# Emitting the input transposes of a sandwich block one tile later in the first attention's epilogue

## Chip, cores, metric

The kernel runs on one Trainium2 chip, on its 8 cores, one batch element of 2048 tokens on each. No data pass between the cores. The metric is device time in microseconds (us) of the slowest core.

## What is computed

The reference is one layer with two attentions and an expert stage. Cut to what matters:

```python
x = x + layernorm(attn(layernorm(x)))          # 16 heads of 64, causal, S = 2048, D = 1024
y = layernorm(x)
z = layernorm(y) * ln1_g + ln1_b               # goes into the second attention
y = y + attn2(z)                               # same shape
y = y + moe(layernorm(y) * ln2_g + ln2_b)      # 8 experts of 1024 -> 4096 -> 1024, gelu, top 2
out = x + layernorm(y)
```

All eight experts are computed for every token and weighted with the gate, which is zero for six of them.

## The kernel before

The program is written out by hand for five queues (TensorE, VectorE, ScalarE, GpSimd, SyncE); `kb.em` appends an instruction to one queue, `kb.wt`, `kb.consume` and `kb.reuse` append the waits. No scheduler moves anything: each engine works in the order in which the Python code emits.

A first stage normalizes the input tile by tile (16 tiles `tt` of 128 tokens), transposes it on TensorE and keeps it in T1, with the features on the partitions. Then comes `emit_attention` (L400), once for the first attention and once for the second. It projects K (L422) and V (L454) for all tokens, and then goes over four query blocks `qs` of 512 tokens. In a block it

- projects Q (L494): 8 groups of 8 matmuls of 512 columns, into the four PSUM banks `pb[0..3]` by turns, each evacuated by ScalarE (L504);
- runs 8 head pairs: scores (L567, masks L578), exponentials on ScalarE (L594), products with V (L615, L621, L625), and an epilogue of each pair (L511 to L545);
- for its four tiles multiplies with the output weights (L660: 16 matmuls, two halves of 8, into banks 0 and 1 or 2 and 3 by turns), and calls the epilogue `epi` of the tile: `epi1` (L672) in the first attention, `epi2` (L727) in the second.

`epi1` is a long chain for one tile: VectorE adds the bias into the buffer scrY (L679, twice), takes the layernorm statistics (`ln_stats`, L252: L256, L257, L258 on VectorE, then Ln and Exp at L260 and L261 on ScalarE), normalizes into scrZ (L690), adds the residual x that a DMA brought (L695), spills the sum x1 to memory, takes statistics a second time, copies mean and scale (L703, L704), and normalizes into scrY again (L706). Last `transpose8` (L265) transposes the eight 128x128 parts of scrY on TensorE (L273), four into bank 4 and four into bank 5, and ScalarE moves them from there into T1 (L718), where the second attention finds its input. There is one scrY: the next tile's first L679 waits until the transposes have read it. T1's part of this query block has been read by the block's Q projection by then.

Every VectorE and ScalarE instruction that is emitted as serial also waits for the one before it on its own engine. `load_bias_bcast` (L341), between the two attentions, brings a bias row by DMA into the buffer RSTG, spreads it over the partitions by two matmuls (L348; a float matmul has two records) into banks 4 and 5, and VectorE copies them out (L357). It is called twice, and the second DMA waits for the first copies.

The expert stage (L953 on) follows the second attention and a normalizing stage; neither is touched.

Of the kernel before, what the change touches and what calls it, by code (L numbers as in the profile page):

```python
# [92 lines left out]
def build_nc():  # L93
# [33 lines left out]
    with ExitStack() as ctx:  # L127
# [30 lines left out]
        kb = KB()  # L158
# [8 lines left out]
        scrY = T5[:, 5120:6144]  # L167
# [39 lines left out]
        r_afm = [Res() for _ in range(NQS)]  # L207
# [9 lines left out]
        r_scrY = Res()  # L217
# [16 lines left out]
        def dma(e, dst, src, res=None, waits=(), dkey=None):  # L234
            for w in waits:
                kb.wt(e, w)
            if res is not None:
                kb.reuse(e, res)
            if dkey is None:
                if res is not None:  # L240
                    dkey = dkeys.setdefault(id(res), "d%d" % len(dkeys))
                else:
                    anon_ctr[0] += 1
                    dkey = "a%d" % anon_ctr[0]
            tok = kb.emd(e, lambda E, d=dst, s=src: E.dma_start(out=d, in_=s), dkey)  # L245
            if res is not None:
                kb.produce(res, tok)
            return tok
# [122 lines left out]
        for tt in range(NT):  # L371
# [3 lines left out]
            m, s, tok_s = ln_stats(xr, waits=(tokd,))  # L375
# [8 lines left out]
            qs = tt // 4  # L384
# [12 lines left out]
                kb.produce(r_afm[qs], [("v", kb.cnt["v"]), ("s", kb.cnt["s"])])  # L397

        spill_toks = []
        def emit_attention(wq_h, wk_h, wv_h, wout_h, bq8c, bkc, epi, first):  # L400
            wsrc = lambda w: w.rearrange("(kc p) d -> p kc d", p=128)
            tok_wq = dma("g", wq_sb.rearrange("p (kc d) -> p kc d", d=1024), wsrc(wq_h), res=r_wq)
            for rr, half_res in ((0, r_whalfA), (1, r_whalfB)):
# [3 lines left out]
                        kb.reuse("g", rc)  # L407
                dma("g", dstA, wsrc(wk_h)[:, rr * 4:(rr + 1) * 4, :], res=half_res)
            tok_wo = dma("g", wo_sb.rearrange("p (kc d) -> p kc d", d=1024), wsrc(wout_h), res=r_wo)

            for c in range(NPAIR):
                kb.reuse("v", r_kfm[c])
# [72 lines left out]
            for qs in range(NQS):  # L485
                kb.reuse("v", r_qsl)
                for c in range(NPAIR):
# [18 lines left out]
                        func=AF.Identity, bias=bq8c[:, c:c + 1], scale=0.125), inc=1, serial=False)  # L506
                    kb.used(r_pb[bank], tv)
                kb.produce(r_qsl, ("s", kb.cnt["s"]))

                nkt = 4 * qs + 4  # L510
                def emit_pair_epilogue(p, rbT, rbb):  # L511
# [137 lines left out]
                for i in range(4):  # L649
                    tt = qs * 4 + i  # L650
                    banks = (2 * (i % 2), 2 * (i % 2) + 1)
                    toks = []
                    for ds in range(2):
                        bank = banks[ds]
                        kb.reuse("t", r_pb[bank])
                        kb.consume("t", r_wo)
                        tk = None
                        for c in range(NPAIR):
                            kb.consume("t", r_ctx[c])
                            tk = kb.em("t", lambda E, c=c, i=i, ds=ds, bank=bank: E.matmul(  # L660
                                out=pb[bank][:],
                                lhsT=ctxsb[:, c * 512 + i * 128:c * 512 + i * 128 + 128],
                                rhs=wo_sb[:, c * 1024 + ds * 512:c * 1024 + ds * 512 + 512],
                                start=(c == 0), stop=(c == NPAIR - 1)), inc=(1 if c == NPAIR - 1 else 0))
                        for c in range(NPAIR):
                            kb.used(r_ctx[c], tk)
                        kb.used(r_wo, tk)
                        kb.produce(r_pb[bank], tk)
                        toks.append(tk)
                    epi(tt, banks, toks)  # L670

        def epi1(tt, banks, toks):  # L672
            qs = tt // 4
            kb.consume("v", r_bob)
            kb.reuse("v", r_scrY)
            ty = None
            for ds in range(2):
                kb.wt("v", toks[ds])
                ty = kb.em("v", lambda E, ds=ds, b=banks[ds]: E.scalar_tensor_tensor(  # L679
                    out=scrY[:, ds * 512:(ds + 1) * 512], in0=pb[b][:], scalar=1.0,  # L680
                    in1=bob[:, ds * 512:(ds + 1) * 512], op0=OP.mult, op1=OP.add), inc=1)
                kb.used(r_pb[banks[ds]], ty)
                kb.used(r_bob, ty)
            kb.produce(r_scrY, ty)
            m, s, tok_s = ln_stats(scrY)
            sl = tt % 2
            xr = T7[:, sl * 1024:(sl + 1) * 1024]
            tokd = dma("q", xr, x_r[tt], res=r_xr[sl])
            kb.wt("v", tok_s)
            tz = scrz_write(lambda E: E.tensor_scalar(  # L690
                out=scrZ, in0=scrY, scalar1=bn2[:, 0:1], scalar2=tstat[:, 1:2],
                op0=OP.subtract, op1=OP.mult))
            kb.used(r_scrY, tz)
            kb.wt("v", tokd)
            tx1 = kb.em("v", lambda E, xr=xr: E.tensor_tensor(  # L695
                out=xr, in0=scrZ, in1=xr, op=OP.add), inc=1)
            scrz_used(tx1)
            tok_sp = dma("q", x1s_r[tt], xr, waits=(tx1,))
            spill_toks.append(tok_sp)
            kb.used(r_xr[sl], tok_sp)  # L700
            m, s, tok_s = ln_stats(xr, waits=(tx1,))
            kb.wt("v", tok_s)
            kb.em("v", lambda E, tt=tt: E.tensor_copy(out=m1s1[:, tt:tt + 1], in_=bn2[:, 0:1]))  # L703
            tms = kb.em("v", lambda E, tt=tt: E.tensor_copy(out=m1s1[:, 16 + tt:17 + tt], in_=tstat[:, 1:2]), inc=1)  # L704
            kb.reuse("v", r_scrY)
            t1 = kb.em("v", lambda E, xr=xr, tt=tt: E.tensor_scalar(  # L706
                out=scrY, in0=xr, scalar1=m1s1[:, tt:tt + 1], scalar2=m1s1[:, 16 + tt:17 + tt],
                op0=OP.subtract, op1=OP.mult), inc=1)
            kb.produce(r_scrY, t1)
            kb.used(r_xr[sl], t1)  # L710

            def evac_h1(c, pap, eng, tt=tt):
                if eng == "v":
                    return kb.em("v", lambda E, c=c, pap=pap: E.tensor_scalar(
                        out=T1[:, c * 2048 + tt * 128:c * 2048 + tt * 128 + 128], in0=pap,
                        scalar1=PPB[:, 32 + c:33 + c], scalar2=PPB[:, 40 + c:41 + c],
                        op0=OP.mult, op1=OP.add), inc=1, serial=False)
                return kb.em("s", lambda E, c=c, pap=pap: E.activation(  # L718
                    out=T1[:, c * 2048 + tt * 128:c * 2048 + tt * 128 + 128], in_=pap,
                    func=AF.Identity, scale=PPB[:, 32 + c:33 + c],  # L720
                    bias=PPB[:, 40 + c:41 + c]), inc=1, serial=False)

            transpose8(scrY, t1, evac_h1, src_res=r_scrY, engines=("s", "s"))
            if tt % 4 == 3:
                kb.produce(r_afm[qs], [("v", kb.cnt["v"]), ("s", kb.cnt["s"])])

        def epi2(tt, banks, toks):  # L727
            kb.consume("v", r_bob)
# [94 lines left out]
        for tt in range(NT):  # L823
# [17 lines left out]
            m, s, tok_s = ln_stats(u_sl(tt, 0, 1024), waits=(tu,))  # L841
# [21 lines left out]
            if pend_gm[0] is not None:  # L863
# [4 lines left out]
                       src_res=r_t2s, engines=("s", "s"))  # L868
# [244 lines left out]
```

How the kernel before makes its waits and increments, by code:

```python
        def runner(eng, e):  # L1040
            for fn, inc in kb.ops[e]:
                if isinstance(fn, tuple):
                    if fn[0] == "WAIT":
                        eng.wait_ge(sems[fn[1]], fn[2])
                    elif fn[0] == "DMA":
                        instr = fn[1](eng)
                        instr.then_inc(sems[fn[2]], 16)
                    continue
                instr = fn(eng)
                if inc:
                    instr.then_inc(sems[e], inc)
```

## Time and profile before

| | us |
|---|---|
| three timed runs | 6350.97, 6714.02, 6923.64 |
| their median | 6714.02 |
| the profiled execution, its own time | 6344.19 |
| its span, slowest core (core 1) | 6342.6 |
| spans of the eight cores | 6326.8 to 6342.6 |
| TensorE busy | 5590.4 (88%) |
| VectorE busy | 1407.7 (22%) |
| ScalarE busy | 1607.1 (25%) |

The span runs from the first to the last instruction of a core; the execution's own time has 1.6 us more. The clock is the share of TensorE's full clock that was granted, 1.0 for 2.4 GHz and 0.5 for 1.2 GHz; over a stretch it is a mean of the two. In the rows an engine's name with a q is its queue, which issues DMAs; "idle before <-releaser" in brackets is how long the engine had stood still and what ended that.

### The profile page before, as it was taken

Reading aid. Unit: us, or ns where it says so; the run is one execution under the profiler, and the core shown is the slowest. Engines: PE = TensorE matmul, PEld = TensorE weight load, DVE = VectorE, ACT = ScalarE, POOL = GpSimd, SP = SyncE. Lnnn points to the kernel's source line nnn. Section 1 sums busy time; section 2 is a strip of 40 time slices with the busy share of each in tenths; the row PEclk is TensorE's granted clock in tenths of the full one; section 3 lists DMA queues with packets and bytes.
Section 4 is the critical chain, followed back from the end, with each engine's and each line's share of the span. In section 5 each row is a group of like instructions: output and inputs, shape, how many; then the busy total and the mean of one; then the engine's idle time right before and its main releaser. Section 6 shows DMA issues by size and latency. Waiting matters only on the chain.

```text
span 6342.6 us, 62715 instructions; the slowest of 8 cores (6326.8 to 6342.6 us)
## 1 busy us (share of the span) xinstructions
PE 5590.4 (88%) x23458; PEld 2241.2 (35%) x23458; DVE 1407.7 (22%) x2208; ACT 1607.1 (25%) x2387; POOL 150.5 (2%) x177
## 2 busy tenths in 40 slices
PE   2868677768888846999999999999999999999996
PEld 1322222232222223444444444444444344344342
DVE  3331211132111142212212211221221121121125
ACT  1034344402444532121121121122112112112111
POOL 0000000000000000000000000000000000000000
PEclk9978788888888867999999999999999999999999
DMA  4100001020001033132123123123123123113113
GB/s 94 21 27 0 27 11 30 17 47 14 4 14 27 1 113 54 27 43 38 27 37 44 27 33 48 27 30 50 27 31 50 27 30 51 27 27 54 27 14 113
DMA packets 195663, 223.51 MB, mean 35 GB/s; under 512 B 6238, under 2 KB 137758, under 8 KB 195370
## 3 DMA queue, kind: packets, MB, share of 16 engines
q0 software_dynamic: 175824, 151.02, 17.2%
q1 hardware_dynamic: 19546, 68.48, 3.4%
q8 instruction: 196, 3.21, 0.2%
q14 instruction: 97, 0.79, 0.0%
HBM read 345.33 MB, written 25.17 MB: 58 GB/s over the span
## 4 chain that ended last, share of the span: by engine, by line
PE 84%; DVE 7%; DMA 3%; issue 3%; ACT 3%; DVEq 0%; ACTq 0%; SPq 0%; POOL 0%; POOLq 0%
PE pw L974 27%; PE pw L1005 14%; PE pbO L1005 7%; PE pbE L1005 7%; PE pbO L625 4%; PE pbE L615 4%; PE pbE L621 3%; PE pw L567 3%; PE pw L578 2%; PE pw L1012 2%; PE pw L660 2%; PE pw L494 2%; PE pw L422 2%; PE pw L454 2%; PE pbO L1012 1%
## 5 line engine op out<-in xcount | busy, mean ns | idle before, releaser
L974 PE MATMUL pw<-T 128*128 128x512 bf16 x8192 | 1775.4, 379 | 1.3 <-DMA T<-L_ffn_exp_W 1.3
L987 ACT ACTIVATE T<-pw,T 128x512 bf16<-128x512 f32 x1024 | 705.1, 689 | 3079.5 <-PE pw L974 3079.5
L974 PEld LDWEIGHTS pw<-T 128*128 128x128 bf16 x8192 | 800.4, 98 | 972.7 <-issue 11.3
L1005 PE MATMUL pw<-T 128*128 128x512 bf16 x4096 | 937.5, 379 | 19.2 <-DVE T L1022 19.2
L594 ACT ACTIVATE T<-pw 128x1024 bf16<-128x1024 f32 x640 | 620.1, 1022 | 599.6 <-PE pw L578 300.6
L1022 DVE SCALAR_TENSOR_TENSOR T<-pbE,T 128x512 f32<-128x512 f32 x256 | 192.3, 751 | 2038.4 <-PE pbE L1005 1509.7
L1005 PEld LDWEIGHTS pw<-T 128*128 128x128 bf16 x4096 | 389.6, 98 | 571.2 <-issue 119.6
L1022 DVE SCALAR_TENSOR_TENSOR T<-pw,T 128x512 f32<-128x512 f32 x512 | 383.9, 751 | 631.1 <-PE pw L1005 358.6
L1005 PE MATMUL pbE<-T 128*128 128x512 bf16 x2048 | 484.3, 379 | 19.9 <-DVE T L1022 19.9
L1005 PE MATMUL pbO<-T 128*128 128x512 bf16 x2048 | 484.4, 379 | 0.0
L273 PE MATMUL pw<-T 128*128 128x128 f32 x384 | 93.1, 424 | 312.0 <-DVE T L706 169.0
L567 PE MATMUL pw<-T 64*128 64x512 bf16 x1280 | 252.6, 443 | 116.3 <-ACT T L533 99.1
L615 PE MATMUL pbE<-T 128*65 128x512 bf16 x640 | 282.6, 442 | 31.7 <-DVE T L540 22.9
L1005 PEld LDWEIGHTS pbE<-T 128*128 128x128 bf16 x2048 | 195.3, 98 | 292.2 <-issue 65.1
L515 DVE COPY T<-pbE 1x512 f32<-1x512 f32 x64 | 44.1, 689 | 1129.6 <-PE pbO L625 1086.7
L1005 PEld LDWEIGHTS pbO<-T 128*128 128x128 bf16 x2048 | 195.1, 98 | 275.1 <-issue 48.5
L625 PE MATMUL pbO<-T 128*64 128x512 bf16 x640 | 283.6, 443 | 0.0
L621 PE MATMUL pbE<-T 128*1 128x512 bf16 x640 | 265.1, 414 | 0.0
L1022 DVE SCALAR_TENSOR_TENSOR T<-pbO,T 128x512 f32<-128x512 f32 x256 | 192.3, 751 | 316.9 <-PE pbO L1005 180.4
L245 POOL DMA_DIRECT2D T<-L_ffn_exp_W x160 | 139.8, 876 | 4680.0 <-PE pw L974 3629.8
L273 PEld LDWEIGHTS pw<-T 128*128 128x128 f32 x384 | 75.3, 223 | 327.9 <-issue 327.9
L578 PE MATMUL pw<-T 128*128 128x512 bf16 x512 | 173.1, 423 | 0.0
(105 smaller groups left out, 2433.8 us busy)
## 6 DMA issues: line engine op xcount, KB each, us to landing
T<-L_ffn_exp_W POOLq DMA_DIRECT2D x32, 2048.0 KB, 22.3
T<-L_ffn_exp_W POOLq DMA_DIRECT2D x128, 512.0 KB, 6.0
T<-xcore SPq DMA_DIRECT2D x32, 512.0 KB, 5.0
T<-x1s SPq DMA_DIRECT2D x32, 512.0 KB, 3.6
x1s<-T SPq DMA_DIRECT2D x16, 512.0 KB, 3.9
atts<-T SPq DMA_DIRECT2D x16, 512.0 KB, 2.7
T<-atts SPq DMA_DIRECT2D x16, 512.0 KB, 4.2
out<-T SPq DMA_DIRECT2D x16, 512.0 KB, 2.7
```

What stands on the lines that cost most here:

```text
L273: tk = kb.em("t", lambda E, c=c, j=j, b=bank: E.transpose(out=ptf[b][:, j * 128:(j + 1) * 128], in_=src1024[:, c * 128:(c + 1) * 128], ide ...
L567: tks[head] = kb.em("t", lambda E, p=p, kt=kt, tsr=tsr, j01=j01, base=base, diag=diag: E.matmul(out=pw[tsr][:, j01 * 512:(j01 + 1) * 512], ...
L578: tks[head] = kb.em("t", lambda E, tsr=tsr, j01=j01, jv=jv: E.matmul(out=pw[tsr][:, j01 * 512:(j01 + 1) * 512], lhsT=identb, rhs=masksA[:, ...
L594: te = kb.em("s", lambda E, slot=slot, tsr=tsr: E.activation(out=pring[slot], in_=pw[tsr][:], func=AF.Exp), inc=1, serial=False)
L615: tk_e = kb.em("t", lambda E, p=p, kt=kt, pr=pr_e, nkt=nkt: E.matmul(out=pbE[0:65, :], lhsT=T4[:, kt * 1032 + p * 129: kt * 1032 + p * 129 ...
L621: tk_s = kb.em("t", lambda E, kt=kt, pr=pr_o, nkt=nkt: E.matmul(out=pbE[96:97, :], lhsT=ones_b[:, 0:1], rhs=pr, start=(kt == 0), stop=(kt ...
L625: tk_o = kb.em("t", lambda E, p=p, kt=kt, pr=pr_o, nkt=nkt: E.matmul(out=pbO[64:128, :], lhsT=T4[:, kt * 1032 + p * 129 + 65: kt * 1032 + ...
L974: tk = kb.em("t", lambda E, sub=sub, ts_=ts_, kc=kc, slw=slw, bank=bank: E.matmul(out=pb[bank][:], lhsT=w1r[slw][:, kc * 256 + sub * 128:k ...
L987: tg = kb.em("s", lambda E, hc=hc, ts_=ts_, e=e, hq=hq, bank=bank: E.activation(out=gmv[:, hc * 2048 + ts_ * 512:hc * 2048 + ts_ * 512 + 512],
L1005: tk = kb.em("t", lambda E, tt=tt, ds=ds, hc=hc, bank=bank, idx=idx, hq=hq: E.matmul(out=g4[bank], lhsT=gmv[:, hc * 2048 + tt * 128:hc * 2 ...
L1012: tk = kb.em("t", lambda E, ds=ds, e=e, bank=bank: E.matmul(out=g4[bank], lhsT=ones_f[0:1, 0:128], rhs=B2R[0:1, (e % 2) * 1024 + ds * 512: ...
L1022: tv = kb.em("v", lambda E, tt=tt, ds=ds, e=e, bank=bank: E.scalar_tensor_tensor(out=u_sl(tt, ds * 512, ds * 512 + 512), in0=g4[bank], sca ...
```

## The change

The eight transposes and their evacuations are no longer emitted at the end of `epi1`. They are wrapped into a function `t8` and kept in `pend_t8`. `flush_t8` emits what is kept. It is called behind the output projection of the next tile and ahead of that tile's epilogue, behind the Q projection of each query block and ahead of its scores, and at the start of `emit_attention`, ahead of the K projection. In the first call of `emit_attention`, and all through the second one's loops, there is nothing kept. The tile's chain on VectorE is the same, instruction for instruction.

```diff
--- before.py
+++ after.py
@@ -397,6 +397,12 @@
                 kb.produce(r_afm[qs], [("v", kb.cnt["v"]), ("s", kb.cnt["s"])])
 
         spill_toks = []
+        pend_t8 = [None]
+
+        def flush_t8():
+            if pend_t8[0] is not None:
+                pend_t8[0]()
+                pend_t8[0] = None
         def emit_attention(wq_h, wk_h, wv_h, wout_h, bq8c, bkc, epi, first):
             wsrc = lambda w: w.rearrange("(kc p) d -> p kc d", p=128)
             tok_wq = dma("g", wq_sb.rearrange("p (kc d) -> p kc d", d=1024), wsrc(wq_h), res=r_wq)
@@ -407,6 +413,7 @@
                         kb.reuse("g", rc)
                 dma("g", dstA, wsrc(wk_h)[:, rr * 4:(rr + 1) * 4, :], res=half_res)
             tok_wo = dma("g", wo_sb.rearrange("p (kc d) -> p kc d", d=1024), wsrc(wout_h), res=r_wo)
+            flush_t8()
 
             for c in range(NPAIR):
                 kb.reuse("v", r_kfm[c])
@@ -506,6 +513,7 @@
                         func=AF.Identity, bias=bq8c[:, c:c + 1], scale=0.125), inc=1, serial=False)
                     kb.used(r_pb[bank], tv)
                 kb.produce(r_qsl, ("s", kb.cnt["s"]))
+                flush_t8()
 
                 nkt = 4 * qs + 4
                 def emit_pair_epilogue(p, rbT, rbb):
@@ -667,6 +675,7 @@
                         kb.used(r_wo, tk)
                         kb.produce(r_pb[bank], tk)
                         toks.append(tk)
+                    flush_t8()
                     epi(tt, banks, toks)
 
         def epi1(tt, banks, toks):
@@ -720,9 +729,12 @@
                     func=AF.Identity, scale=PPB[:, 32 + c:33 + c],
                     bias=PPB[:, 40 + c:41 + c]), inc=1, serial=False)
 
-            transpose8(scrY, t1, evac_h1, src_res=r_scrY, engines=("s", "s"))
-            if tt % 4 == 3:
-                kb.produce(r_afm[qs], [("v", kb.cnt["v"]), ("s", kb.cnt["s"])])
+            def t8(tt=tt, qs=qs, t1=t1, evac_h1=evac_h1):
+                transpose8(scrY, t1, evac_h1, src_res=r_scrY, engines=("s", "s"))
+                if tt % 4 == 3:
+                    kb.produce(r_afm[qs], [("v", kb.cnt["v"]), ("s", kb.cnt["s"])])
+
+            pend_t8[0] = t8
 
         def epi2(tt, banks, toks):
             kb.consume("v", r_bob)
```

The inserted lines shift the numbers: L494, L504, L567, L594, L660 and L718 are L501, L511, L575, L602, L668 and L727 in the changed kernel, K's L422 is L429. Lines up to L398 keep theirs.

TensorE, the end of the first query block and the start of the second, before (L523 and L526 belong to the last pair's epilogue, L660 is the output projection, L273 the transposes, L494 the Q projection, L567 the scores):

```order
L523 MATMUL pw<-T 64x512
L526 MATMUL pw<-T 64x512
L660 MATMUL pw<-T 128x512 x16
L273 MATMUL pw<-T 128x128 x8
L660 MATMUL pw<-T 128x512 x16
L273 MATMUL pw<-T 128x128 x8
L660 MATMUL pw<-T 128x512 x16
L273 MATMUL pw<-T 128x128 x8
L660 MATMUL pw<-T 128x512 x16
L273 MATMUL pw<-T 128x128 x8
L494 MATMUL pw<-T 128x512 x64
L567 MATMUL pw<-T 128x512 x8
```

The same place in the changed kernel:

```order
L531 MATMUL pw<-T 64x512
L534 MATMUL pw<-T 64x512
L668 MATMUL pw<-T 128x512 x32
L273 MATMUL pw<-T 128x128 x8
L668 MATMUL pw<-T 128x512 x16
L273 MATMUL pw<-T 128x128 x8
L668 MATMUL pw<-T 128x512 x16
L273 MATMUL pw<-T 128x128 x8
L501 MATMUL pw<-T 128x512 x64
L273 MATMUL pw<-T 128x128 x8
L575 MATMUL pw<-T 128x512 x8
```

Two tiles of output projection (32 matmuls) now stand ahead of the first transposes, and the last tile's transposes stand behind the 64 matmuls of the Q projection. The other blocks read alike.

ScalarE at the same place, before (L260 and L261 are Ln and Exp of the statistics, L718 the evacuations of the transposes, L504 those of the Q projection, L594 the first exponentials):

```order
L718 ACTIVATE T<-pw,PPB 128x128 x8
L260 ACTIVATE T<-T 128x1
L261 ACTIVATE T<-T 128x1
L260 ACTIVATE T<-T 128x1
L261 ACTIVATE T<-T 128x1
L718 ACTIVATE T<-pw,PPB 128x128 x8
L504 ACTIVATE T<-pw,PPB 128x512 x8
L594 ACTIVATE T<-pw 128x1024 x10
```

And in the changed kernel:

```order
L727 ACTIVATE T<-pw,PPB 128x128 x8
L260 ACTIVATE T<-T 128x1
L261 ACTIVATE T<-T 128x1
L260 ACTIVATE T<-T 128x1
L261 ACTIVATE T<-T 128x1
L511 ACTIVATE T<-pw,PPB 128x512 x8
L727 ACTIVATE T<-pw,PPB 128x128 x8
L602 ACTIVATE T<-pw 128x1024 x10
```

The last tile's evacuations moved behind the eight Q evacuations, whose direct predecessor is now the last tile's second Exp (L261).

TensorE between the two attentions, before (L348 are the two bias rows, L422 the K projection):

```order
L660 MATMUL pw<-T 128x512 x16
L273 MATMUL pw<-T 128x128 x8
L660 MATMUL pw<-T 128x512 x16
L273 MATMUL pw<-T 128x128 x8
L348 MATMUL pw<-RSTG,T 128x512 x4
L422 MATMUL pw<-T 128x512 x256
```

And in the changed kernel:

```order
L668 MATMUL pw<-T 128x512 x16
L273 MATMUL pw<-T 128x128 x8
L668 MATMUL pw<-T 128x512 x16
L273 MATMUL pw<-T 128x128 x8
L348 MATMUL pw<-RSTG,T 128x512 x4
L273 MATMUL pw<-T 128x128 x8
L429 MATMUL pw<-T 128x512 x256
```

Here the last transposes went from ahead of the bias matmuls to behind them; the first ones of this piece are those of the tile before.

## Rows read from the trace of the kernel before

**Rows 1.** The page: the span, and the chain that ended last by engine.
```profile
span 6342.6 us, 62715 instructions; the slowest of 8 cores (6326.8 to 6342.6 us)
...
PE 84%; DVE 7%; DMA 3%; issue 3%; ACT 3%; DVEq 0%; ACTq 0%; SPq 0%; POOL 0%; POOLq 0%
```

**Rows 2.** Windows: stretch, its length, busy by engine, clock, DMA share, GB/s.
```profile
488.00:640.00 152.00, 123.37 (x412) 30.40 (x412) 20.72 (x30) 69.95 (x78) 0.00 (x0) 0.83 0.00 0
...
726.00:920.00 194.00, 165.11 (x589) 42.49 (x587) 20.72 (x30) 103.00 (x113) 0.00 (x0) 0.87 0.00 1
920.00:988.00 68.00, 25.33 (x90) 12.48 (x89) 32.31 (x54) 13.93 (x42) 0.00 (x0) 0.70 0.21 62
...
1005.50:1237.70 232.20, 202.92 (x736) 52.83 (x736) 20.72 (x30) 132.65 (x142) 1.29 (x2) 0.89 0.09 13
...
1460.00:2263.00 803.00, 691.96 (x2469) 192.78 (x2466) 109.84 (x159) 369.31 (x413) 1.76 (x2) 0.86 0.06 16
```

**Rows 3.** Groups by line: the transposes; busy, mean ns, idle before, releasers.
```profile
L273 PE MATMUL pw<-T 128*128 128x128 f32 x384 | 93.1, 424 | 312.0 <-DVE T L706 169.0 <-DVE T L847 77.0 <-DVE T L378 66.0
```

**Rows 4.** Timeline, third query block, second tile: start, length, engine, line.
```profile
941.20 0.69 DVE L679 SCALAR_TENSOR_TENSOR T<-pw,T 128x512 f32<-128x512 f32 x1 [5.53 <-PE pw L660]
942.92 0.69 DVE L679 SCALAR_TENSOR_TENSOR T<-pw,T 128x512 f32<-128x512 f32 x1 [1.04 <-PE pw L660]
943.72 0.69 DVE L256 BATCH_NORM_STATS2 T<-T 128x6 f32<-128x512 f32 x1
...
951.02 0.20 ACT L261 ACTIVATE T<-T 128x1 f32<-128x1 f32 x1
...
951.91 0.81 DVE L706 TENSOR_SCALAR T<-T 128x1024 f32<-128x1024 f32 x1
953.29 1.94 PE L273 MATMUL pw<-T 128*128 128x128 f32 x8 [10.55 <-DVE T L706]
954.48 2.91 ACT L718 ACTIVATE T<-pw,PPB 128x128 bf16<-128x128 f32 x8 [3.26 <-PE pw L273]
...
958.41 0.69 DVE L679 SCALAR_TENSOR_TENSOR T<-pw,T 128x512 f32<-128x512 f32 x1 [5.69 <-PE pw L660]
```

**Rows 5.** Timeline, from that block's third transposes to the next block's first exponential.
```profile
970.55 1.94 PE L273 MATMUL pw<-T 128*128 128x128 f32 x8 [10.59 <-DVE T L706]
...
989.45 15.15 PE L494 MATMUL pw<-T 128*128 128x512 bf16 x64
992.61 0.69 ACT L504 ACTIVATE T<-pw,PPB 128x512 bf16<-128x512 f32 x1 [0.80 <-PE pw L494]
994.34 0.69 ACT L504 ACTIVATE T<-pw,PPB 128x512 bf16<-128x512 f32 x1 [1.04 <-PE pw L494]
...
1006.22 3.79 ACT L594 ACTIVATE T<-pw 128x1024 bf16<-128x1024 f32 x4 [0.83 <-PE pw L567]
```

**Rows 6.** Timeline, from the last block's third transposes to K of attention two.
```profile
1288.18 1.94 PE L273 MATMUL pw<-T 128*128 128x128 f32 x8 [10.64 <-DVE T L706]
...
1300.94 0.37 SPq L245 DMA_DIRECT2D RSTG<-L_ffn_bv  x1
...
1303.83 0.81 DVE L706 TENSOR_SCALAR T<-T 128x1024 f32<-128x1024 f32 x1
...
1309.62 3.75 PE L348 MATMUL pw<-RSTG,T 1*128 1x512 f32 x4 [2.43 <-ACT T L718]
...
1314.32 0.24 SPq L245 DMA_DIRECT2D RSTG<-L_ffn_bp  x1
1319.49 3.75 PE L348 MATMUL pw<-RSTG,T 1*128 1x512 f32 x4 [6.12 <-DMA RSTG<-L_ffn_bp]
...
1323.17 56.97 PE L422 MATMUL pw<-T 128*128 128x512 bf16 x256
```

**Rows 7.** Timeline, TensorE alone: the first block's Q projection, right behind V.
```profile
287.05 13.98 PE L494 MATMUL pw<-T 128*128 128x512 bf16 x64
```

## The prediction

> **What bounds the kernel now.** First the head of the page and its chain: the span is 6342.6 us, and 84% of the chain that ended last lies on TensorE, 7% on VectorE [rows 1]. So a change on TensorE counts where TensorE waits, and it must be found where. The windows show the place: in the stretch 920 to 988, the four tile epilogues of the third query block, TensorE is busy for 25.33 of 68 us at a clock of 0.70, and DMA at a share of 0.21; in the attention stretches around it TensorE is busy for 80 to 90% of the time [rows 2]. The groups by line name the wait: before the transposes at L273 TensorE stood still for 169.0 us until L706, the last VectorE step of `epi1` [rows 3]. That is 16 tiles (4 blocks of 4) by 10.6 us.
>
> The timeline of one tile shows the loop [rows 4]. VectorE starts L679 at 941.20 and ends L706 at 951.91 + 0.81 = 952.72, so the chain of a tile takes 11.52. The transposes start 0.57 later (953.29) and take 1.94. The next tile's output projection follows, and the next L679 is at 958.41: the period is 17.21. In it the output projection and the chain never lie beside each other, although the projection needs nothing of the chain: it only stands behind the transposes in TensorE's list. That is what the change alters.
>
> **The change part by part.** Nothing is computed less: the same matmuls, evacuations and VectorE steps, in another order on TensorE and, at three block ends, on ScalarE. VectorE's order is the same. I follow tiles 0 to 3 of a block.
>
> *Inside a block.* The output projection of tile 1 runs during the chain of tile 0; the transposes of tile 0 then start when they started before, since L706 releases them in both kernels. From there the period is new. When the transposes of tile t have read scrY, both halves of the output projection of tile t+1 have long ended, and the chain starts at once. The second L679 no longer waits 1.04 for TensorE [rows 4] but follows after the usual 0.11 (943.72 less 943.61): the chain is 11.52 - 0.93 = 10.6. From L706's end to the transposes 0.57. For the release of scrY: ScalarE starts on the first four transposes 1.19 behind the start of eight (954.48 less 953.29), four take 0.97, so the second four are free at about 2.15. Period: 10.6 + 0.57 + 2.15 = 13.3 instead of 17.2. Gain 3.9 a period, and there are two of them from the first to the third transposes of a block: 7.8. The output projection itself is hidden: 4.9 us (3.2 from the transposes' end at 955.23 to the first L679, which waits for its first half, and 1.73 for the second) in a gap of 11.2. The x tile for L695 is no new wait: its buffer turns over every second tile and its DMA is issued by SP behind the spill of the tile before, still a whole chain ahead of its use.
>
> *Block ends 0, 1 and 2.* Before, from the start of the third transposes (970.55) to the next block's first exponential (1006.22) it is 35.67 [rows 5]: output projection, chain of tile 3, transposes, 15.15 of Q projection, scores. Now, with 0 at the start of the third transposes: the chain of tile 3 starts at 2.15, and the Q projection at 1.94 beside it. Q's evacuations L504 stand behind the chain's Ln and Exp in ScalarE's list. From the first L679 to the end of the second L261 it is 951.22 - 941.20 = 10.02, less the 0.93 saved: 9.1. So ScalarE is free for L504 at 11.3. TensorE fills its four banks by about 1.94 + 8.2 = 10.1 (a group of 8 takes 1.73, the spacing of the L504 rows, and Q's slow start 15.15 - 13.98 = 1.2 [rows 5, 7]), waits 2.0 until the first L504 (0.69) has ended at 12.1, and runs the other four groups until 12.1 + 4 x 1.73 = 19.0. The chain ended at 12.75, so the transposes start at 19.0 with nothing to wait for. Their evacuations start 1.19 later and take 2.91 [rows 4]: 23.1. The exponentials are behind them on ScalarE, so the first starts at 23.15; the scores (under 2 us) are hidden beside the evacuations. 35.67 - 23.15 = 12.5 gained.
>
> Here a rule of the Trainium skill can be weighed. In the rows each L504 starts 0.8 to 1.04 idle behind the last, that is, on its own matmuls; no row of before shows one held by a Ln or Exp ahead of it. The page "TensorE: Matmul & The Clock Gate", section "Architectural detail: the array is 16× 32×32, not 1× 128×128", says that ScalarE and VectorE take their instructions strictly first in, first out. By that rule the stall of 2.0 stands; if ScalarE could pass a waiting Exp, each block end would gain 2.0 more, 6 in all.
>
> *Between the attentions.* Before, from the third transposes of the last block (1288.18) to the K projection (1323.17) it is 35.0 [rows 6]. Now the last chain ends at 12.75 by the same count. The first bias row's DMA is issued 3.7 ahead of the end of L706 (1304.64 less 1300.94), and a row takes 5.17 from issue to its matmul (1319.49 less 1314.32): matmuls at 12.75 + 1.5 = 14.2. Before, they waited for the evacuations instead. From the first L348 to the end of the second it is 1323.24 - 1309.62 = 13.6; then the deferred transposes, 1.94, and K at 29.8. Gain 5.2. K's first three groups read other blocks' columns, so the last evacuations (2.2 beyond the transposes) hide behind 5 us of matmuls. K's weights wait for the last output projection, which is now issued a tile earlier.
>
> *Sum.* 4 x 7.8 + 3 x 12.5 + 5.2 = 31.2 + 37.5 + 5.2 = 73.9. All of it is on the path: attention stages, the second attention and the experts follow in order with no fixed date. Against the profiled execution, 6344.19 - 73.9 = 6270.3. That execution stands 370 below the median of the three runs shown, 6714.02, and 7 below the fastest, 6350.97; the forecast is for executions like these.
>
> *Bounds of what I can't read.* Q's slow start: 1.2 may vanish if the shorter standstill ahead (13.3 - 1.94 - 4.9 = 6.4 instead of 10.6) keeps the clock up; 3 x 1.2 = 3.5 more gain, or it may be paid twice, 3.5 less. The transposes' start varies from 0.26 to 0.6 in the rows, 12 x 0.3 = 3. The stall of 2.0 may be absent (6 more) or reach to the chain's end (1.5 a block, 4.5 less). The larger unknown is the granted clock in the untouched attention stretches, 0.83, 0.87, 0.89 and 0.86 over 1381 us, 1183 of them TensorE [rows 2]: weighted with their lengths 0.863, from which they differ by up to 0.03 with the same code. A shift of 0.02 in all of them is 1183 x 0.02 / 0.863 = 27 us either way. I take zero, since the 64 Q matmuls that run ahead of the scores still do.
>
> **The rivals.**
> *The deferral at block ends gives nothing.* Q fills its banks and then waits for ScalarE until the chain is over, and the transposes with their evacuations only move into the way of the exponentials. For it: the order of ScalarE, with the Ln and Exp ahead of Q's evacuations. Against it: four banks cover 8.2 of the 9.4 until ScalarE is free. If it held, only the inner periods would be left: 31.2 gained, 6313.
>
> *The clock falls (slower than before).* The attention stretches start at another moment against whatever sets the clock. A fall by 0.054 from 0.863 costs 1183 x 0.054 / 0.863 = 74, all of the gain; below 0.81 the change is a loss. At 0.78 it is 114 lost, 6344 + 40 = 6384. For it: in the epilogue stretch the clock is 0.70 [rows 2], so TensorE can be held at 1.2 GHz near it. Against: the epilogue becomes denser, not sparser.
>
> *The clock rises.* By the same count 0.02 more gives 27, with the bounds above 6235. In the row, Q behind the standstill starts at low clock, and Q right behind V does not [rows 5, 7]. The Trainium skill, "TensorE: Matmul & The Clock Gate", section "What's actually happening", states that rest throttles the array and activity releases it. By that rule a fuller epilogue can only help; the traces agree as far as the 1.2 us of Q.
>
> *It does not do what it says.* If some wait kept the next output projection from starting early, the time would be 6344. Against: its banks are the other pair, its inputs are complete, and the printed order has it ahead.
>
> **How the numbers follow.** Forecast, 6270: 0.79. Block ends give nothing, 6313: 0.07. Clock rises, 6235: 0.08. No effect, 6344: 0.02. Clock falls, 6384 or so: 0.04. The range takes the clock bound and the first rival: 6220 to 6328. Two per cent, about what a measurement of this kernel can tell from no change, is 127 us: faster means under 6217, reached only if the clock rises by over 0.04, 0.04; slower means over 6471, 0.03; within it 0.93.
>
> **What would show it.** In the changed profile: the idle before L273 until L706 shrinks from 169.0 to about 74 (in each block 5.7 for the first, twice 6.4, none for the last); transposes inside a block 13.3 apart; Q's L511 first starting some 11 behind the third transposes, with TensorE idle about 2 in Q; the first exponential of a block 23 behind the third transposes; K 30 behind. The forecast is wrong if L679 still waits for TensorE by over a microsecond inside a block, if the transposes behind Q wait for VectorE, or if the attention stretches differ in clock by more than 0.02.

## Result and profile after

| | before | after |
|---|---|---|
| median of 21 timed runs | 6644.21 | 6352.72 |
| lowest timed run | 6341.25 | 6272.19 |
| profiled execution, own time | 6344.19 | 6270.76 |
| its span, slowest core | 6342.6 | 6269.2 |
| mean of the eight cores' spans | 6335.6 | 6261.6 |

The ratio after to before is 0.9902, with an interval of 0.9876 to 0.9929; by the verdict's 2% that is no change. Timed again later, it was 0.9882 (0.9866 to 0.9899). The medians hold runs in which the cores of a die ran at a lower granted clock (in the changed kernel's median run cores 0 to 3 had 0.922 to 0.924 and spans of 6312.0 to 6351.2, the others 0.937 to 0.938 and 6262.0 to 6271.8), and the ratio leaves all but the mildest of those out: that is why the medians lie 291 apart and the profiled executions 73.4. The forecast of 6270 meets the profiled execution to a microsecond; the median, 6352.72, lies above the range of 6220 to 6328.

The page of the changed kernel, beside [rows 1]: the chain has the same shape.

```profile
span 6269.2 us, 62253 instructions; the slowest of 8 cores (6251.6 to 6269.2 us)
...
PE 83%; DVE 7%; DMA 4%; issue 3%; ACT 3%; DVEq 0%; ACTq 0%; SPq 0%; POOL 0%; POOLq 0%
```

The group of the transposes, beside [rows 3] (L715 was L706):

```profile
L273 PE MATMUL pw<-T 128*128 128x128 f32 x384 | 90.6, 414 | 225.1 <-DVE T L715 81.2 <-DVE T L859 78.1 <-DVE T L378 65.9
...
L688 DVE SCALAR_TENSOR_TENSOR T<-pw,T 128x512 f32<-128x512 f32 x32 | 22.1, 692 | 41.2 <-PE pw L273 30.9 <-PE pw L668 9.1
```

The wait for L715 fell from 169.0 to 81.2. L688 (was L679) now starts when the transposes have read scrY, 30.9 in all, and for 9.1 when the output projection is done, at each block's first tile.

The timeline of the third block on core 1, the core of the rows of before, beside [rows 4] (start, length, engine, line). A block given by its number is counted from 0, so the third block is block 2:

```profile
897.53 1.94 PE L273 MATMUL pw<-T 128*128 128x128 f32 x8 [7.14 <-DVE T L715]
...
899.26 5.09 PE L668 MATMUL pw<-T 128*128 128x512 bf16 x16
899.65 1.49 DVE L688 SCALAR_TENSOR_TENSOR T<-pw,T 128x512 f32<-128x512 f32 x2 [2.37 <-PE pw L273]
...
909.43 0.81 DVE L715 TENSOR_SCALAR T<-T 128x1024 f32<-128x1024 f32 x1
910.82 1.94 PE L273 MATMUL pw<-T 128*128 128x128 f32 x8 [6.47 <-DVE T L715]
```

The two L688 lie close together, the output projection (L668) beside the chain. From L688 to the end of L715 it is 10.59, from transposes to transposes 13.29.

The end of the block, beside [rows 5]:

```profile
924.11 1.94 PE L273 MATMUL pw<-T 128*128 128x128 f32 x8 [6.29 <-DVE T L715]
...
925.84 8.90 PE L501 MATMUL pw<-T 128*128 128x512 bf16 x32
...
935.11 0.20 ACT L261 ACTIVATE T<-T 128x1 f32<-128x1 f32 x1
935.22 2.41 ACT L511 ACTIVATE T<-pw,PPB 128x512 bf16<-128x512 f32 x4
...
936.04 7.07 PE L501 MATMUL pw<-T 128*128 128x512 bf16 x32 [1.30 <-ACT T L511]
...
942.94 1.04 PE L273 MATMUL pw<-T 128*128 128x128 f32 x8
...
943.79 2.90 ACT L727 ACTIVATE T<-pw,PPB 128x128 bf16<-128x128 f32 x8
...
946.53 1.99 ACT L602 ACTIVATE T<-pw 128x1024 bf16<-128x1024 f32 x2
947.74 1.04 PE L575 MATMUL pw<-T 64*128 64x512 bf16 x4 [3.10 <-ACT T L602]
```

Q runs 32 matmuls, stops for 1.30 until the second L261 has let the first L511 through, and runs the other 32. The deferred transposes follow at once, in 1.04 instead of 1.94. Their evacuations start at 943.79, and the first exponential follows them at 946.53: 22.42 behind the third transposes, where it was 35.67.

And the passage to the second attention, beside [rows 6]:

```profile
1216.63 0.89 POOL L245 DMA_DIRECT2D T<-L_ffn_Wp  x1
...
1217.97 1.19 SPq L245 DMA_DIRECT2D T<-xcore  x1
...
1222.29 1.94 PE L273 MATMUL pw<-T 128*128 128x128 f32 x8 [6.94 <-DVE T L715]
...
1231.61 1.23 DVE L704 TENSOR_TENSOR T<-T 128x1024 f32<-128x1024 f32 x1 [2.09 <-DMA T<-xcore]
...
1233.29 0.37 SPq L245 DMA_DIRECT2D RSTG<-L_ffn_bv  x1
...
1242.23 3.75 PE L348 MATMUL pw<-RSTG,T 1*128 1x512 f32 x4 [18.00 <-DMA RSTG<-L_ffn_bv]
...
1246.93 0.24 SPq L245 DMA_DIRECT2D RSTG<-L_ffn_bp  x1
1248.78 3.75 PE L348 MATMUL pw<-RSTG,T 1*128 1x512 f32 x4 [2.80 <-DMA RSTG<-L_ffn_bp]
...
1254.42 1.91 PE L429 MATMUL pw<-T 128*128 128x512 bf16 x4
```

The first line is the load of the second attention's output weights (2 MB). It goes out 5.7 ahead of the third transposes; before, it went out 7.8 behind them:

```profile
1295.94 0.89 POOL L245 DMA_DIRECT2D T<-L_ffn_Wp  x1
```

L704 now waits for the x tile, 2.09 here and 0.5 to 2.1 on the eight cores, which before did not. The first bias row takes 8.9 from its issue to its matmul, and that is not new: [rows 6] have 8.7 (1309.62 less 1300.94), and over the eight cores of the kernel before it was 7.8 to 9.5. The row there names the evacuations as what ended the wait. But the matmul needs bank 4 alone, whose four evacuations end 19.8 behind the third transposes on every core, while the matmul starts at 20.6 to 22.3; on core 5 the row names the DMA. The second row takes 1.85, where it took 5.17. K starts 32.1 behind the third transposes, not 29.8.

Where the time went, on core 1, from the starts of these groups in the two timelines:

| stretch | before | after | gain | forecast |
|---|---|---|---|---|
| output projection to third transposes, 4 blocks | 203.8 | 169.9 | 33.9 | 31.2 |
| third transposes to first exponential, 3 | 106.9 | 67.3 | 39.6 | 37.5 |
| third transposes to K | 35.0 | 32.1 | 2.9 | 5.2 |
| first exponential to output projection, blocks 1 to 3 | 576.4 | 583.0 | -6.6 | 0 |
| ahead of the first output projection | 401.1 | 402.1 | -1.0 | 0 |
| from K to the end | 5019.4 | 5010.5 | 8.9 | 0 |

The sum is 77.7, the difference of this core's spans (6342.6 and 6264.9). The last row is no effect that I can place: cores of one kernel differ by 16 to 18 us in their spans, and this one was before's slowest. In the means of the eight cores the gains are 33.5, 39.6, 3.2, -5.0, 0.3 and 2.4, and their sum is 74.0.

### The profile page after: what moved, and what is told of

Read it like the earlier page. It is cut to its first block, busy times and chain, and to the rows that moved or that the text cites. A ratio compares the mean times of both kernels' runs of the same rounds, so it can differ in the third digit from the quotient of the medians.

```text
span 6269.2 us, 62253 instructions; the slowest of 8 cores (6251.6 to 6269.2 us)
## 1 busy us (share of the span) xinstructions
PE 5555.2 (89%) x23020; PEld 2239.6 (36%) x23458; DVE 1407.0 (22%) x2208; ACT 1602.3 (26%) x2387; POOL 150.5 (2%) x177
## 4 chain that ended last, share of the span: by engine, by line
PE 83%; DVE 7%; DMA 4%; issue 3%; ACT 3%; DVEq 0%; ACTq 0%; SPq 0%; POOL 0%; POOLq 0%
PE pw L986 27%; PE pw L1017 14%; PE pbO L1017 7%; PE pbE L1017 7%; PE pbO L633 4%; PE pbE L623 4%; PE pbE L629 4%; PE pw L575 3%; PE pw L586 2%; PE pw L1024 2%; PE pw L429 2%; PE pw L461 2%; PE pw L501 1%; DMA T<-L_ffn_exp_W 1%; PE pbO L1024 1%
## 5 line engine op out<-in xcount | busy, mean ns | idle before, releaser
L986 PE MATMUL pw<-T 128*128 128x512 bf16 x8026 | 1766.5, 379 | 12.1 <-DMA T<-L_ffn_exp_W 2.6
L1017 PE MATMUL pw<-T 128*128 128x512 bf16 x4008 | 928.9, 379 | 16.2 <-DVE T L1034 10.6
L602 ACT ACTIVATE T<-pw 128x1024 bf16<-128x1024 f32 x640 | 620.1, 1021 | 597.1 <-PE pw L575 299.7
L1017 PE MATMUL pbE<-T 128*128 128x512 bf16 x2006 | 489.3, 385 | 22.2 <-DVE T L1034 19.9
L575 PE MATMUL pw<-T 64*128 64x512 bf16 x1280 | 252.9, 444 | 119.0 <-ACT T L541 98.9
L623 PE MATMUL pbE<-T 128*65 128x512 bf16 x640 | 285.3, 446 | 30.2 <-DVE T L548 22.4
L523 DVE COPY T<-pbE 1x512 f32<-1x512 f32 x64 | 44.1, 689 | 1104.4 <-PE pbO L633 1066.3
L273 PE MATMUL pw<-T 128*128 128x128 f32 x384 | 90.6, 414 | 225.1 <-DVE T L715 81.2
L586 PE MATMUL pw<-T 128*128 128x512 bf16 x457 | 156.6, 417 | 10.6 <-issue 10.6
L273 PEld LDWEIGHTS pw<-T 128*128 128x128 f32 x384 | 73.2, 218 | 241.6 <-issue 241.0
```

Of the source, the lines that this page charges most:

```text
L273: tk = kb.em("t", lambda E, c=c, j=j, b=bank: E.transpose(out=ptf[b][:, j * 128:(j + 1) * 128], in_=src1024[:, c * 128:(c + 1) * 128], ide ...
L575: tks[head] = kb.em("t", lambda E, p=p, kt=kt, tsr=tsr, j01=j01, base=base, diag=diag: E.matmul(out=pw[tsr][:, j01 * 512:(j01 + 1) * 512], ...
L586: tks[head] = kb.em("t", lambda E, tsr=tsr, j01=j01, jv=jv: E.matmul(out=pw[tsr][:, j01 * 512:(j01 + 1) * 512], lhsT=identb, rhs=masksA[:, ...
L602: te = kb.em("s", lambda E, slot=slot, tsr=tsr: E.activation(out=pring[slot], in_=pw[tsr][:], func=AF.Exp), inc=1, serial=False)
L623: tk_e = kb.em("t", lambda E, p=p, kt=kt, pr=pr_e, nkt=nkt: E.matmul(out=pbE[0:65, :], lhsT=T4[:, kt * 1032 + p * 129: kt * 1032 + p * 129 ...
L986: tk = kb.em("t", lambda E, sub=sub, ts_=ts_, kc=kc, slw=slw, bank=bank: E.matmul(out=pb[bank][:], lhsT=w1r[slw][:, kc * 256 + sub * 128:k ...
```

## Experiments

Times are those of the profiled execution, beside 6344.19 before and 6270.76 for the change, unless said. Where no ratio is given, it is one profile against one. By the verdict's 2% no edit alone is a change, and of all together the interval reaches over 0.98. "To the exponential" is from the third transposes of a block to the next block's first exponential on core 1.

**Inner tiles alone.** The last tile of a block is transposed at once.

```diff
             pend_t8[0] = t8
+            if tt % 4 == 3:
+                flush_t8()
```

> The last tile of each block is transposed at once, as before; only tiles 0 to 2 are deferred. Theory (the output projection is hidden behind the chain, and what is left of the gain comes from Q beside the last chain): three periods of 17.2 become 13.3 in each of the four blocks, 4 x 3 x 3.9 = 47 of gain, a profiled time near 6297; the third transposes to the next first exponential 31.8 (35.67 less 3.9). Rival (deferral past Q is worth nothing): as fast as the change itself, 6271.

Measured 6295.75, ratio 0.992 (0.9901 to 0.9939). To the exponential 31.8 to 32.6, the period of 13.3 now three times in a block:

```profile
938.54 1.94 PE L273 MATMUL pw<-T 128*128 128x128 f32 x8 [6.30 <-DVE T L715]
...
951.83 1.94 PE L273 MATMUL pw<-T 128*128 128x128 f32 x8 [11.35 <-DVE T L715]
...
953.57 15.98 PE L501 MATMUL pw<-T 128*128 128x512 bf16 x64
```

TensorE stands for 11.35 ahead of the last transposes, and Q comes behind them. The rival is out: deferring the last tile too is worth 25 us.

**Block ends alone.**

```diff
             pend_t8[0] = t8
+            if tt % 4 != 3:
+                flush_t8()
```

> Only the last tile of each block is deferred, behind Q or behind the bias rows; tiles 0 to 2 are transposed at once. Theory: periods stay 17.2; from the third transposes the output projection ends at 6.8, the chain's second Exp at 15.1, Q's first four groups are done at about 14, Q ends at 22.8, first exponential at 27.0 instead of 35.67: 3 x 8.7 = 26, and 1 to 2 between the attentions, 6317. The two gains add up to that of the change, 47 + 27 = 74. Rival (Q's evacuations wait behind the chain so long that nothing is won): 6344.

Measured 6326.83, ratio 0.9966 (0.9952 to 0.9979): 17 of gain instead of 27. To the exponential it was 26.1 to 26.3, better than the 27.0 expected. Q's wait is longer here than in the change, 2.30 and not 1.30: its first four groups take 7.07 at a clock of 1.00, in the change 8.90 at 0.79, so it stands ready sooner:

```profile
969.01 2.41 ACT L511 ACTIVATE T<-pw,PPB 128x512 bf16<-128x512 f32 x4
969.83 7.07 PE L501 MATMUL pw<-T 128*128 128x512 bf16 x32 [2.30 <-ACT T L511]
```

But K started 36.6 behind the third transposes, 1.6 later than before, and the attention stretches of blocks 1 to 3 took 584.0 on core 1 where they had taken 576.4. K is late because of the bias row. Here the load of the output weights goes out as late as before, and the row takes 8.9 to its matmul, with the DMA named:

```profile
1272.61 0.89 POOL L245 DMA_DIRECT2D T<-L_ffn_Wp  x1
...
1277.61 0.37 SPq L245 DMA_DIRECT2D RSTG<-L_ffn_bv  x1
...
1286.48 3.75 PE L348 MATMUL pw<-RSTG,T 1*128 1x512 f32 x4 [15.15 <-DMA RSTG<-L_ffn_bv]
```

The row holds its matmul with the last transposes ahead of it or without, so taking them away from there wins nothing, and behind the rows they cost their own time. From the third transposes to K the means of the eight cores are 34.3 before, 29.1 with the inner tiles alone, 36.3 with the block ends alone and 31.1 with both: at this place the deferral loses 2.0, and the early output projection gains 5.2.

Both gains are real (48 and 17), but their sum is 8 short of the 73 of both. In the means of the eight cores about half of what is missing lies in the attention stretches, which lost 2.7, 6.9 and, with both, 5.0.

**Two buffers.** A chain no longer waits for the transposes of the tile before it.

```diff
         def epi1(tt, banks, toks):
             qs = tt // 4
+            yb = (scrY, sscrW)[tt % 2]
+            r_yb = (r_scrY, r_sscr[0])[tt % 2]
...
-                transpose8(scrY, t1, evac_h1, src_res=r_scrY, engines=("s", "s"))
+                transpose8(yb, t1, evac_h1, src_res=r_yb, engines=("s", "s"))
```

> The change, and scrY alternates between two buffers, so that a chain no longer waits for the transposes of the tile before. Theory (the period is the chain 10.6 + 0.57 + transposes 2.15, held together by the single scrY): the period falls from 13.3, but not to 10.6, since the transposes' eight evacuations stand ahead of the next Ln and Exp on ScalarE and end 4.7 behind the chain's end where the first Ln is due at 3.5: 11.8. Gain over the change 4 x 2 x 1.5 and about 1 at each block end: 15, 6256. Rival (something else than scrY holds the period, as the output projection or the x DMA): period 13.3, 6271.

Measured 6254.87, ratio 0.9852 (0.9833 to 0.9872), periods of 11.8 to 11.9 (the transposes at 893.22 and 905.05 below). The row of L260 has no idle time ahead of it: ScalarE came straight from the evacuations, and L701 waits 1.72 instead of 0.91.

```profile
893.22 1.94 PE L273 MATMUL pw<-T 128*128 128x128 f32 x8 [7.14 <-DVE T L717]
894.40 2.92 ACT L729 ACTIVATE T<-pw,PPB 128x128 bf16<-128x128 f32 x8 [2.94 <-PE pw L273]
...
897.42 0.30 ACT L260 ACTIVATE T<-T 128x1 f32<-128x1 f32 x1
...
898.18 0.81 DVE L701 TENSOR_SCALAR T<-T 128x1024 f32<-128x1024 f32 x1 [1.72 <-ACT T L261]
...
905.05 1.94 PE L273 MATMUL pw<-T 128*128 128x128 f32 x8 [5.01 <-DVE T L717]
```

So scrY held the period, and behind it stood ScalarE's order.

**Two buffers, evacuations behind the first statistics.**

```diff
-                    flush_t8()
                     epi(tt, banks, toks)
...
             m, s, tok_s = ln_stats(yb)
+            flush_t8()
```

> As with two buffers, and the deferred transposes are emitted between the two statistics of the next tile's epilogue, which alters only ScalarE's order: the first Ln and Exp come ahead of the eight evacuations. Theory: period 10.6, the bare chain; gain over the change 4 x 2 x 2.7 + 3 x 1.3 + 2.7 = 28, 6243. Rival (ScalarE's order does not matter, or the evacuations now hold up the second Ln and Exp): no faster than with two buffers alone.

Measured 6246.13, ratio 0.9855 (0.9838 to 0.9872). In the third block the transposes start at 888.15, 899.17 and 909.88: the second of these distances is 10.71, nearly the chain and nothing else, and all eight on core 1 lie between 10.66 and 11.22. The profiled executions differ by 9 us in favour of this one (the means of their eight cores by 12.8), the ratios not at all: its five runs lie between 6246.13 and 6265.46, and with intervals of 0.002 to 0.004 the timed runs cannot tell the two apart. The mechanism is shown by the period, its worth is not.

**Bias rows behind K.**

```diff
+            if not first:
+                load_bias_bcast(fb["v"], bvb, r_bvb)
+                load_bias_bcast(fb["p"], bob, r_bob)
             kb.consume("v", r_bvb)
...
-        load_bias_bcast(fb["v"], bvb, r_bvb)
-        load_bias_bcast(fb["p"], bob, r_bob)
         emit_attention(fW["q"], fW["k"], fW["v"], fW["p"], PPB[:, 72:80], PPB[:, 24:32], epi2, False)
```

> The change, with both bias rows between the attentions emitted behind the second attention's K projection instead of ahead of it. Theory (K starts late only because the bias rows and their two DMAs stand ahead of it on TensorE; K's weights are there): K 17.4 less in front, it starts at 17 behind the third transposes of the last block instead of 31.8, and the bias matmuls are hidden in TensorE's wait for V's weights of 15 us: 14 of gain, 6257. Rival (K's weights would be late, or the bias rows delay V as much): K starts no earlier than 25, or V later by what K gained; 6271.

Measured 6256.39. K starts 15.6 behind the third transposes, straight behind the last ones:

```profile
1233.41 1.94 PE L273 MATMUL pw<-T 128*128 128x128 f32 x8 [11.91 <-DVE T L718]
...
1235.15 56.55 PE L429 MATMUL pw<-T 128*128 128x512 bf16 x256
...
1298.82 3.75 PE L348 MATMUL pw<-RSTG,T 1*128 1x512 f32 x4 [5.21 <-DMA RSTG<-L_ffn_bp]
...
1302.50 1.89 PE L464 MATMUL pw<-T 128*128 128x512 bf16 x4
1306.26 3.92 PE L464 MATMUL pw<-T 128*128 128x512 bf16 x11 [1.88 <-DMA T<-L_ffn_Wv]
```

V starts 67.35 behind K, in the changed kernel 67.05. The bias rows cost nothing there, because TensorE waits for V's weights in any case.

**The output weights held back.**

```diff
+            if not first:
+                kb.consume("g", r_bob)
             tok_wo = dma("g", wo_sb.rearrange("p (kc d) -> p kc d", d=1024), wsrc(wout_h), res=r_wo)
```

> The change, with the DMA of the second attention's output weights (2 MB) held until the bias rows are out. Theory (in the changed kernel this load runs into the x tile of tile 15, for which L704 waited 2.10, and into the first bias row, 8.8 from issue to its matmul instead of 5.2): L704's wait goes, the bias row takes 5 or less, and K starts 26 to 28 behind the third transposes instead of 31.8; 6266. Rival (half of K's weights, 1 MB, is enough to delay them, or SP's issue of 2.2 us is to blame): K at 31 to 32 again.

Measured 6263.33. L706 (L704 in the change) no longer waits for x, and the first bias row takes 3.0 from issue to matmul:

```profile
1231.66 1.23 DVE L706 TENSOR_TENSOR T<-T 128x1024 f32<-128x1024 f32 x1
...
1233.33 0.37 SPq L245 DMA_DIRECT2D RSTG<-L_ffn_bv  x1
...
1236.30 3.75 PE L348 MATMUL pw<-RSTG,T 1*128 1x512 f32 x4 [10.04 <-DMA RSTG<-L_ffn_bv]
```

K starts at 24.0, 8 us earlier than in the change (7 in the means of the eight cores). Both waits were collisions with that 2 MB load. The change released it 13.4 us earlier against the third transposes, by issuing the last output projection ahead of them, and that made the wait for x new. The bias row had the load beside it in the kernel before as well; what the earlier release did to the rows was a gain, since the load lands 22.3 behind the third transposes, ahead of the second row, which takes 1.85 and not 5.17.

**Q's evacuations ahead of the second Exp.** The hook runs in `epi1`, between spill and second statistics; the block's loop then leaves out the two groups.

```diff
+                    if first and i == 3 and qs < 3:
+                        mid_hook[0] = lambda qs=qs: [q_group(qs + 1, c) for c in range(2)]
                     epi(tt, banks, toks)
```

> The change, with the first two Q groups of the next block emitted between the two statistics of the last tile, so that on ScalarE two of Q's evacuations stand ahead of the second Ln and Exp; TensorE's order is the same. Theory (the 1.3 us for which Q's fifth group waits are ScalarE's list order alone): the wait is gone, the third transposes to the first exponential 21.1 instead of 22.4, 4 less in all, 6267. Rival (the banks or the last tile's output projection hold Q): the wait stays.

To the exponential 21.2, 21.1 and 21.0 in the three blocks. Q is one piece again:

```profile
955.46 15.82 PE L500 MATMUL pw<-T 128*128 128x512 bf16 x64
...
959.88 0.67 ACT L510 ACTIVATE T<-pw,PPB 128x512 bf16<-128x512 f32 x1
...
964.35 0.29 ACT L260 ACTIVATE T<-T 128x1 f32<-128x1 f32 x1 [2.65 <-DVE T L258]
```

The wait of 1.30 was ScalarE's list order and nothing else; here the Trainium skill's rule that the forecast weighed ("TensorE: Matmul & The Clock Gate", "Architectural detail: the array is 16× 32×32, not 1× 128×128") agrees with the trace. The execution's own 6290.9 says nothing of 4 us: cores 0 and 1 span 6279.2 and 6289.3, and they reach the first output projection at 428.5 and 432.4, the other six at 397 to 402, ahead of everything that the edit touches. Those six span 6252.9 to 6262.2, in the change all eight 6251.6 to 6269.2.

**All together.** Two buffers with late evacuations, bias rows behind K, and the last tile's transposes inside Q:

```diff
                     kb.used(r_pb[bank], tv)
+                    if c == 4:
+                        flush_t8()
                 kb.produce(r_qsl, ("s", kb.cnt["s"]))
```

> Two buffers with late evacuations, bias rows behind K, and the last tile's transposes emitted behind Q's fifth group instead of behind its eighth. Theory: the gains add up: 28 from the buffers, 14 from the bias rows, and 1.7 at each block end since the evacuations now fit between Q's; 6271 - 28 - 14 - 5 = 6224, a ratio of 0.981 to the kernel before. Rival (the gains overlap, as both shorten the last block's end): 6240.

Measured 6221.12. Third transposes to the first exponential 19.0, to K 12.3. Its ratio of 0.985 (0.9787 to 0.9913) was too wide to read, so it ran again:

> The kernel with all edits again, for its ratio. Theory: 6220, a ratio of 0.980 to the kernel before. Rival: the first profile was a lucky one, 6235.

Measured 6220.71, five runs of 6220.71 to 6225.48, ratio 0.9804 (0.9789 to 0.9819): 124 us less than before, 50 less than the change.

**Both kernels once more.** The attention stretches had grown by 1 to 3 us each; was that the change?

> The kernel before, once more profiled. Its four attention stretches (first exponential of a block to its output projection) were 154.9, 190.0 and 231.5 us in blocks 1 to 3 on core 1, and 1 to 3 us longer in the changed kernel, at a granted clock lower by 0.01 to 0.03. Theory (this belongs to the execution and not to the change): they differ by 1 to 4 us from the first profile here too. Rival (the change lengthens them): within 0.5 us of the first profile.

> The changed kernel, once more profiled and timed in the same session as the next run. Theory: 22.4 from the third transposes to the first exponential and periods of 13.3 again, as they hang on waits; attention stretches another mix; 6270 plus or minus 5. Rival (the change's attention stretches are longer by themselves): 158, 191 and 234 to within 0.5.

My theory fell. In two profiles of each kernel, on all eight cores, the stretch of block 2 took 190.0 before and 190.8 to 191.1 after, that of block 3 231.5 to 231.6 and 233.6 to 233.7. Only block 1 mixes (154.8 to 158.8, and 156.9 to 158.3). The changed kernel gave 6272.83 in the profile; its ratio beside the kernel before is 0.9882, the second figure given above. The windows of block 3's first 10 us, before and after (columns as in [rows 2]):

```profile
1006.00:1011.00 5.00, 3.45 (x17) 0.96 (x15) 0.00 (x0) 3.86 (x5) 0.03 (x1) 1.00 0.90 118
1011.00:1016.00 5.00, 5.00 (x21) 1.41 (x20) 0.00 (x0) 3.90 (x5) 0.00 (x0) 1.00 0.99 145
```

```profile
946.00:951.00 5.00, 3.26 (x9) 0.71 (x9) 0.00 (x0) 4.45 (x6) 0.00 (x0) 0.56 0.90 126
951.00:956.00 5.00, 5.00 (x17) 1.09 (x16) 0.00 (x0) 2.11 (x3) 0.00 (x0) 0.76 1.06 188
```

Before, the block opens at full clock, 2.4 GHz. In the changed kernel the granted clock is 0.56, mostly the level of 1.2 GHz, after TensorE stood for 3.10 behind the late evacuations, and the first pair's epilogue comes 25.6 behind the first exponential instead of 23.8. That the 3.10 alone does it is not shown: with all edits together there is no such wait (1.25 at that place), and yet that block too opens at 0.69 and 0.63, with 26.0 for the first pair; with the inner tiles alone it opens at 1.00, with 23.5. What sets the clock at a block's start stays open. Nor is it shown that the time is lost there: on core 1 the first pair's epilogue is late by 2.8, 0.8 and 1.8 in blocks 1 to 3, most of the 6.6, but in block 2 of the first profile of the kernel before it comes at 18.5 on cores 5 and 6 and at 19.9 on the other six, and the stretch is 190.0 on all of them.

## Why the prediction was right, and where it was wrong

**The mechanism** held inside the blocks: the output projection only stood behind the transposes in TensorE's list. A period of 13.3 was forecast and 13.29 measured; the chain 10.6 and 10.59; the wait for L706, "about 74", was 81.2. The gain there, 33.9 and not 31.2, was mis-sized on the side of the kernel before: its period was 17.2 in the tile that I read, but 17.76 in the mean of the eight on core 1, so a period gained 4.4 and not 3.9; 1.3 in all went again ahead of the blocks' first transposes.

**The block ends** gave 0.7 more than forecast each, 22.4 instead of 23.15. The deferred transposes take 1.04 and not 1.94, because they now come straight behind 64 matmuls, at a clock of 1.00: I had used one duration for both places. Their first evacuation starts 0.85 behind them and not 1.19, and the exponential 2.74 behind that and not 2.9. Q ended at 18.83 and not 19.0. Its wait was 1.30, not 2.0, but that gave next to nothing: its first four groups took 8.90 and not 8.2, and the wait ended where ScalarE let it, at 11.9 instead of 12.1.

**Between the attentions** the claim that the x tile "is no new wait" failed: it cost 2.0, since moving the last output projection had moved the release of a weight load on POOL's queue. The step "a row takes 5.17 from issue to its matmul" failed as well, and with it "Before, they waited for the evacuations instead": the 5.17 is the second row's, the first took 8.9, and 8.7 before, as the difference in [rows 6] says. That cost 3.8. The second row, priced at 5.17 too, took 1.85, which gave 3.3 back. Cost of all: 2.3 of the 5.2 forecast here; holding one load back gave 8 on core 1.

**The rival "the deferral at block ends gives nothing"** was priced wrongly, 31.2 and 6313. Where the last tile is transposed at once, its period shrinks as well: three periods, 47, which is 6297. The experiment has 6295.75.

**The clock** was right as the largest unknown, but it was put at zero with a reason that failed: "since the 64 Q matmuls that run ahead of the scores still do". They do, and the mean clock of the stretches still fell, in block 1 from 0.828 to 0.797 on core 1, in blocks 2 and 3 from 0.865 to 0.857 and from 0.889 to 0.876. The first is past the 0.02 that the forecast named as a sign of being wrong, though there the eight cores differ by as much in one kernel (0.800 to 0.828 before). The loss of 6.6 in the attention stretches is within the 27 allowed, but for blocks 2 and 3 it repeats from run to run, so it belongs to the change.

**The number.** 6270 was forecast, for "executions like these", that is, like the profiled one; that execution has 6270.76, and the ratio on 6344.19 gives 6282 (the nine times in it hold 6312.35 and 6334.25; the other seven are 6272.19 to 6275.85). That 6270.76 meets the sum so closely is partly luck: in the means of the eight cores 76.3 was gained where 73.9 was forecast, 5.0 was lost in the attention stretches, and 2.7 came from stretches that the change does not touch. But the median of the timed runs is 6352.72, outside the range. The step that failed is the last one of the sum: I noted that the profiled execution stood 370 below the median shown, 6714.02, and then took that execution's time for the one that would be measured. As a range for the median, 6220 to 6328 was far too narrow: the three runs shown already spread over 573, eight times the gain, and 13 of the changed kernel's 21 timed runs lie above 6328. Its lower end was not worked out either: the bounds that I list add up to about 40 downward, which is 6230.

## What to carry to other kernels

Where an in-order engine waits for a long chain on others, look at what stands directly behind that wait in its list: if it needs nothing of the chain, emitting the dependent work one step later hides it, for a few lines of code. Then ask which single buffer now joins the two loops (here scrY, 2.7 us a period), and on which other engine's list the moved work now stands ahead of something urgent. Moving an instruction also moves the release of every DMA that waits for it: look for what is in flight in the new place, and in the old. A row that names an engine as what ended a wait is checked against the time when that engine was done: here a wait put down to evacuations that had ended 1.7 earlier was one for a bias row of 8.7 us.

## What was not expected of the hardware

- Eight float transposes took 1.94 in the opening stage, where the clock column reads 1.00 for the whole of it (67 to 158 us), and 1.94 at a clock of 0.50 in the epilogues, but 1.04 behind a long run of matmuls at 1.00. In the opening stage the duration is that of the lower level, against the column.

```profile
67.00:158.00 91.00, 30.43 (x127) 24.88 (x128) 49.88 (x122) 19.24 (x90) 0.00 (x0) 1.00 0.27 81
942.90:944.00 1.10, 1.08 (x9) 0.80 (x7) 0.00 (x0) 0.80 (x2) 0.35 (x1) 1.00 0.00 0
```

- The attention stretches of blocks 2 and 3 repeat over cores and executions, to 0.1 us in the kernel before and to 0.3 in the changed one, and change by 1 to 3 when other code ahead of them changes.
- A bias row of 4 KB took 8.9 us from issue to its matmul beside a load of 2 MB, 8.7 in the kernel before, and 3.0 without the load.
